# Attention scores from two float32r parts in 64-row tiles of the array, with the stacks loaded by GpSimd

## The reference, cut to what matters

```
Q = norm(x) @ Wq ; K = ctx @ Wk ; V = ctx @ Wv         (16 heads, d_k = 16)
scores = einsum('bhqd,bhkd->bhqk', Q, K) / sqrt(16)     (4 x 16 x 512 x 512)
attn = softmax(scores) ; out = einsum('bhqk,bhkd->bhqd', attn, V)
x = x + tanh(gate) * (out @ Wo)
```

## Time and profile before

| what | us |
|---|---|
| median of 3 runs | 898.56 (896.37 to 900.29) |
| profiled execution, its own time as the span from first to last instruction | 909.3 |
| PE busy, share of the span | 849.0, 93% |
| DVE busy | 618.8, 68% |
| ACT busy | 504.3, 55% |
| POOL busy | 161.1, 18% |
| steps of attention in layer 0 and layer 1, first `key_scores` to last `values` | 61.4 to 255, 518.3 to 715 |

### The profile page before, as it was taken

One profiled execution on the slowest core, in us unless ns is written; L12 is line 12 of the kernel. 1 busy time (PEld: TensorE's weight loads), 2 busy tenths in 40 slices (PEclk: granted clock), 3 DMA queues, 4 the chain that ended last, 5 costly groups with the idle time before them and its releaser, 6 DMA issues.

```text
span 909.3 us, 14428 instructions
## 1 busy us (share of the span) xinstructions
PE 849.0 (93%) x4542; PEld 474.4 (52%) x4543; DVE 618.8 (68%) x1207; ACT 504.3 (55%) x678; POOL 161.1 (18%) x283
## 2 busy tenths in 40 slices
PE   9999999999988999999968999999999989993398
PEld 6543333333468899999844433333334654441387
DVE  5898888888771222233248978888886578698942
ACT  4567777777731122222235667777777674597660
POOL 3241111111264000000151423000005303000000
PEclk9999999999999999999988999999999989997699
DMA  8898466654362111111469663333310000000011
GB/s 296 184 285 235 91 168 171 164 165 127 114 212 93 35 35 35 37 38 38 162 181 239 180 182 73 80 84 83 82 43 2 1 1 1 0 0 1 0 41 52
DMA packets 66558, 91.13 MB, mean 100 GB/s; under 512 B 24134, under 2 KB 50630, under 8 KB 66502
## 3 DMA queue, kind: packets, MB, share of 16 engines
q1 hardware_dynamic: 59196, 67.83, 29.0%
q0 software_dynamic: 5584, 19.93, 6.6%
q10 hardware_dynamic: 1728, 2.75, 0.8%
HBM read 62.64 MB, written 27.44 MB: 99 GB/s over the span
## 4 chain that ended last, share of the span: by engine, by line
PE 80%; DVE 8%; ACT 4%; issue 2%; DMA 2%; another core or an unknown queue 2%; SPq 1%; POOL 1%; DVEq 0%; ACTq 0%; POOLq 0%
PE PS L2197 13%; PE PS L2165 13%; PE PS L2186 12%; PE PS L2356 9%; PE PS L2422 8%; PE PS L2341 8%; PE PS L2443 5%; PE PS L2297 3%; PE PS L2148 1%; PE PS L2211 1%; PE PS L2128 1%; PE PS L2111 1%; PE PS L2175 1%; ACT BIG L1291 1%
## 5 line engine op out<-in xcount | busy, mean ns | idle before, releaser
L1571 DVE TENSOR_REDUCE MX<-PS 128x1 f32<-128x512 f32 x512 | 321.4, 684 | 44.3 <-PE PS L2165 43.6
L1148 ACT ACTIVATE Pt<-PS 128x1024 f32<-128x1024 f32 x256 | 248.1, 1021 | 101.6 <-PE PS L2186 100.7
L2165 PE MATMUL PS<-KSt,BIG 96*128 96x512 bf16 x512 | 175.4, 384 | 3.7 <-DVE bias_row L1458 2.7
L2186 PE MATMUL PS<-BIG,KSt 99*128 99x512 bf16 x512 | 150.5, 380 | 2.1 <-ACT Pt L1148 1.4
L2197 PE MATMUL PS<-Pt,VS 128*17 128x512 f32 x1024 | 137.0, 601 | 0.0
L2165 PEld LDWEIGHTS PS<-KSt,BIG 96*128 96x128 bf16 x512 | 40.6, 97 | 144.5 <-DVE MX L1571 87.3
L2341 PEld LDWEIGHTS PS<-KSt,Pt 128*128 128x128 f32 x736 | 85.6, 192 | 1.9 <-issue 0.8
L2341 PE MATMUL PS<-KSt,Pt 128*128 128x128 f32 x736 | 86.0, 275 | 0.7 <-issue 0.7
L1695 DVE COPY KSt<-PS 128x256 f32<-128x256 f32 x23 | 9.8, 425 | 111.1 <-PE PS L2328 111.1
L2422 PE MATMUL PS<-KSt,BIG 128*128 128x512 f32 x192 | 83.5, 596 | 0.0
L2186 PEld LDWEIGHTS PS<-BIG,KSt 99*128 99x128 bf16 x512 | 49.5, 98 | 56.3 <-ACT Pt L1148 4.9
(11 more groups left out here) (199 smaller groups left out, 1077.4 us busy)
## 6 DMA issues: line engine op xcount, KB each, us to landing
qk_parts<-BIG SPq DMA_DIRECT2D x64, 192.0 KB, 3.7
BIG<-in_w POOLq DMA_DIRECT2D x12, 1024.0 KB, 5.6
BIG<-qk_parts SPq DMA_DIRECT2D x32, 192.0 KB, 3.3
KSt<-qk_parts SPq DMA_DIRECT2D x32, 192.0 KB, 3.8
v_rows<-BIG SPq DMA_DIRECT2D x8, 544.0 KB
VS<-v_rows SPq DMA_DIRECT2D x32, 136.0 KB, 3.0
BIG<-qk_parts SPq DMA_DIRECT2D x32, 128.0 KB, 3.8
KSt<-qk_parts SPq DMA_DIRECT2D x32, 128.0 KB, 3.9
```

The lines of the kernel that those rows point to most:

```text
L1148: act.activation(PP[:, 2 * (kc % 2) + half, :, :].rearrange("p h t -> p (h t)"), ST[half], ACT.Exp, scale=DK ** -0.5).then_inc(exp_done, 1)
L1571: dve.tensor_reduce(MX[:, g % 2, i % TB, i // TB:i // TB + 1], ring(i), AX.X, ALU.max, negate=True).then_inc(max_taken, 1)
L2165: pe.matmul(ring(i), QS[0:ROWS, g, h, qc * P:(qc + 1) * P], KS[0:ROWS, g, h, :], start=True, stop=True).then_inc(max_done, 1)
L2186: last = pe.matmul(ST[half][:, i * S:(i + 1) * S], KS[0:ROWS + PARTS, g, h, kc * P:(kc + 1) * P], QS[0:ROWS + PARTS, g, h, :], start=True, ...
```

## The change

**Two parts instead of three.** Q and K are each kept as two float32r parts: the high part, which ACT writes as float32r, and the rest, which DVE writes as float32r in one instruction. The middle parts of ACT (32 instructions) and the low parts of POOL (26) and DVE (6) are gone. A stack has three pairs of parts, 48 rows, and two rows for the maximum, which is also split in two.

**Half of the array.** 50 rows fit into 64. Of the four heads of a group, heads 0 and 1 lie in partitions 0 to 63 and heads 2 and 3 in partitions 64 to 127, each matmul of `key_scores` and `max_scores` names its half with `tile_position`. The two heads of one ST buffer lie in the same half. `max_scores` takes the halves in turn (`half = i % 2`).

**Loads by POOL.** The stacks, the ones and the rows of the maxima are loaded by DMAs issued from POOL: eight a stack and two for the maxima. SP and ACT issue none of these now. POOL's loop over the sequences is written out. The stored parts are float32, 256 KB a store pair instead of 192 KB; a stack has 768 KB as before.

The diff, cut to its core:

```diff
...
-PARTS = 3
-ROWS = 6 * DK
-RUNS = [(0, 3), (3, 2), (5, 1)]
+PARTS = 2
+ROWS = 3 * DK
+HALF = P // 2
...
+            return PT[:, slot(kind, p, c), r, :]
+
+        STACK_IN = 8 * 16
+
+        def rows_of(half, first, count):
+
+            return slice(HALF * half + first * DK, HALF * half + (first + count) * DK)
+
+        def max_rows_at(half):
+
+            return slice(HALF * half + ROWS, HALF * half + ROWS + PARTS)
+
+        def head_of(i):
+
...
-            def load_stack(layer, b, g, some=range(len(RUNS))):
-                for first, k in [RUNS[i] for i in some]:
-                    dst = slice(first * DK, (first + k) * DK)
-                    for stack, which, parts in ((QS, 0, slice(0, k)), (KS, 1, slice(PARTS - k, PARTS))):
-                        run = qk_dram[layer, which, b, g, parts].rearrange("r (d h) t -> (r d) (h t)", h=G)
-                        sp.dma_start(stack[dst, g, :, :].rearrange("p h t -> p (h t)"), run).then_inc(q_stack[g], 16)
...
             def attention(layer):
-                for j in range(2 * KC):
-                    sp.wait_ge(part_out[j], 32 * B * (layer + 1))
                 sp.wait_ge(v_out, 16 * B * (layer + 1))
                 def batch(n, first, last):
                     for g in range(NG):
                         s = NG * n + g
                         if not last:
-                            sp.wait_ge(st_done, 8 * (s + 1))
-                            load_stack(layer, n + 1 - B * layer, g)
                             sp.wait_ge(pv_done, 4 * (s + 1))
                             load_v(layer, n + 1 - B * layer, g)
...
+                gp.wait_ge(ones_kept, 16)
+                load_ones()
+                first_stacks(0)
                 split_max(0, 0)
...
+            def load_stack(layer, b, g, half):
+                q, k = [qk_dram[layer, which, b, g].rearrange("r (d f h) t -> f r d (h t)", f=2, h=J)[half]
+                        for which in range(2)]
+                gp.dma_start(KS[rows_of(half, 0, 2), g, :, :].rearrange("p j t -> p (j t)"), k).then_inc(q_stack[g], 16)
+                gp.dma_start(QS[rows_of(half, 0, 2), g, :, :].rearrange("p j t -> p (j t)"),
+                             q[0].unsqueeze(0).to_broadcast([2, DK, J * S])).then_inc(q_stack[g], 16)
+                gp.dma_start(QS[rows_of(half, 2, 1), g, :, :].rearrange("p j t -> p (j t)"), q[1]).then_inc(q_stack[g], 16)
+                gp.dma_start(KS[rows_of(half, 2, 1), g, :, :].rearrange("p j t -> p (j t)"), k[0]).then_inc(q_stack[g], 16)
+
+            def load_stacks(layer, b, g):
+                for half in range(2):
+                    load_stack(layer, b, g, half)
+
+            def load_max_rows(n, g):
+
+                gp.wait_ge(max_copied, NG * n + g + 1)
+                gp.wait_ge(q_stack[g], STACK_IN * (n + 1))
+                for half in range(2):
+                    gp.dma_start(QS[max_rows_at(half), g, :, :],
+                                 MR[PARTS * J * TB * half:PARTS * J * TB * (half + 1), g % 2, :]).then_inc(max_rows[g], 16)
+
+            def parts_landed(layer, kind, c):
+                gp.wait_ge(part_out[slot(kind, 0, c)], landed(layer, kind, 0) + 32)
+
+            def first_stacks(layer):
+                for c in range(KC):
+                    parts_landed(layer, "k", c)
+                    parts_landed(layer, "q", c)
+                    load_stacks(layer, 0, 2 * c)
+                    load_stacks(layer, 0, 2 * c + 1)
...
+                s, top = NG * n + g, MX[:, g % 2, :, :].rearrange("p (f j) t -> p f j t", f=2)
                 gp.wait_ge(max_taken, 16 * (s + 1))
                 wait(gp, max_turned, s)
-                gp.tensor_tensor(MP[:, :, 0, :], MX[:, q, :, :], zero, ALU.subtract).then_inc(max_link, 1)
-                gp.wait_ge(max_link, 3 * s + 1)
-                gp.tensor_tensor(MD[:, :, :], MX[:, q, :, :], MP[:, :, 0, :], ALU.subtract).then_inc(max_link, 1)
-                gp.wait_ge(max_link, 3 * s + 2)
-                gp.tensor_tensor(MP[:, :, 1, :], MD[:, :, :], zero, ALU.subtract).then_inc(max_link, 1)
-                gp.wait_ge(max_link, 3 * s + 3)
-                gp.tensor_tensor(MP[:, :, 2, :], MD[:, :, :], MP[:, :, 1, :], ALU.subtract).then_inc(max_parts, 1)
+                gp.tensor_tensor(MP[:, :, 0, :, :].bitcast(F32R), top, zero, ALU.subtract).then_inc(max_link, 1)
+                gp.wait_ge(max_link, s + 1)
+                gp.tensor_tensor(MP[:, :, 1, :, :].bitcast(F32R), top, MP[:, :, 0, :, :], ALU.subtract).then_inc(max_parts, 1)
...
             def attention(layer, between):
 
+                for j in range(2 * KC):
+                    gp.wait_ge(part_out[j], 32 * B * (layer + 1))
+
                 def batch(n, first, last):
                     for g in range(NG):
                         if not (last and g == NG - 1):
                             split_max(n + (g + 1) // NG, (g + 1) % NG)
+                        fresh = g > 0 and not last or g == 0 and not first
+                        if fresh:
+                            gp.wait_ge(st_done, 8 * (NG * n + g))
+                            load_stacks(layer, n + (g > 0) - B * layer, (g - 1) % NG)
+                        if not (last and g == NG - 1):
+                            load_max_rows(n + (g + 1) // NG, (g + 1) % NG)
                         between(n, g, first, last)
-                over_batches(gp, layer, batch)
+                for b in range(B):
+                    batch(B * layer + b, b == 0, b == B - 1)
...
+            def low_part(layer, kind, p, c):
+
+                dve.wait_ge(hi_done, made(layer, kind, p, c) + 1)
                 if layer:
-                    dve.scalar_tensor_tensor(RB[:, c, :], qk_bank(c), bias_of(kind, c),
-                                             part_of(kind, p, c, 0), ALU.add, ALU.subtract).then_inc(r_done, 1)
+                    dve.scalar_tensor_tensor(part_of(kind, p, c, 1).bitcast(F32R), qk_bank(c), bias_of(kind, c),
+                                             part_of(kind, p, c, 0), ALU.add, ALU.subtract).then_inc(lo_done, 1)
                 else:
-                    dve.tensor_tensor(RB[:, c, :], qk_bank(c), part_of(kind, p, c, 0),
-                                      ALU.subtract).then_inc(r_done, 1)
-
-            def rests(layer, kind, p):
-
-                rest_of(layer, kind, p, 0)
-                rest_of(layer, kind, p, 1)
-
...
                 for i in some:
-                    h, qc = i // TB, i % TB
+                    half, j, qc = i % 2, i // 2 % J, i // G
+                    rows = rows_of(half, 0, ROWS // DK)
                     if i == 0:
-                        pe.wait_ge(q_stack[g], 96 * (n + 1))
+                        pe.wait_ge(q_stack[g], STACK_IN * (n + 1))
                     if i == 8 and max_before is not None:
                         pe.wait_ge(max_copied, max_before + 1)
                     elif i == 14 and out_before is not None:
                         pe.wait_ge(o_ready, out_before + 1)
                     else:
                         wait(pe, max_taken, 16 * (NG * n + g) + ring_before(i))
-                    pe.matmul(ring(i), QS[0:ROWS, g, h, qc * P:(qc + 1) * P], KS[0:ROWS, g, h, :],
-                              start=True, stop=True).then_inc(max_done, 1)
+                    pe.matmul(ring(i), QS[rows, g, j, qc * P:(qc + 1) * P], KS[rows, g, j, :], start=True, stop=True,
+                              tile_position=(HALF * half, 0)).then_inc(max_done, 1)
...
 
@@ -2171,20 +2079,19 @@
                 pe.wait_ge(max_parts, s + 1)
                 if ahead is not None:
                     pe.wait_ge(max_taken, 16 * ahead + 4)
-                for t in range(TB):
-                    last = pe.transpose(to[0:PARTS * G, t * P // 2:(t + 1) * P // 2].bitcast(BF16),
...
             def key_scores(s, n, g, kc, half):
 
                 if kc == 0 and half == 0:
-                    pe.wait_ge(max_rows[g], 16 * (n + 1))
+                    pe.wait_ge(max_rows[g], 32 * (n + 1))
                 wait(pe, exp_done, 2 * (4 * s + kc) + half - 1)
-                for i in range(2):
-                    h = 2 * half + i
-                    last = pe.matmul(ST[half][:, i * S:(i + 1) * S], KS[0:ROWS + PARTS, g, h, kc * P:(kc + 1) * P],
-                                     QS[0:ROWS + PARTS, g, h, :], start=True, stop=True)
+                rows = slice(HALF * half, HALF * half + ROWS + PARTS)
+                for j in range(J):
+                    last = pe.matmul(ST[half][:, j * S:(j + 1) * S], KS[rows, g, j, kc * P:(kc + 1) * P],
+                                     QS[rows, g, j, :], start=True, stop=True,
+                                     tile_position=(HALF * half, 0))
                 last.then_inc(st_done, 1)
 
...
```

More of the change, by code:

```diff
@@ L27 @@
 F32 = mybir.dt.float32
+F32R = mybir.dt.float32r
 BF16 = mybir.dt.bfloat16
@@ L82, in build_program @@
         PS = ctx.enter_context(nc.psum_tensor("PS", [P, 8, 512], F32))
```

(20 more changed lines are left out.)

242 lines of the change are left out of this document (58 added, 184 removed).

## The result

The changed kernel took 973.9 us (median of 4 runs, 954.7 to 992.1) against 898.0 before: 1.070 times as long, 95% interval 1.062 to 1.077. The changed kernel is slower, and outside the predicted range of 862 to 930 us. The profiled run is the fastest of the four; the others had a lower mean clock of PE, 0.89 to 0.93 against 0.95, where the kernel before had 0.98.

The account below looks back on a forecast made before the run. PE was taken to bound the kernel, DVE close behind, and POOL's late maxima to set most steps after the change. Steps -20.2 us plus preparation +7.9 gave -12.3, hence 885 us, range 862 to 930.

Parts of the forecast that it names:

- The chain over two steps: Attention steps with stacks: matmuls for the maxima, DVE, POOL's split, ten issues and landing sum to 22.5 us, 11.25 a step.
- a landing of 2.1 us: Last term of the two-step sum: time for the DMA of the maxima to land before the next step's key_scores.
- Issues of POOL: Small direct DMA issues back to back on POOL, ten a step with stacks: 0.80 us each, between bounds 0.74 and 1.28.
- The rival of POOL's issues: POOL's stack issues ahead of the maxima become the bound: 913 us at 1.0 us an issue, 956 at 1.28; chance 15%.
- the rival without overlap: Matmuls in different halves of the array run one after another: +15 us, 914 us; chance 13%.
- half pace: Rival: float32r matmuls on PE take 0.435 us instead of 0.22, giving steps of 15.6 us and 1,030 us; chance 14%.
- 0.44 us a quarter: PE's score matmuls in a step: halves side by side turn eight 0.22 us slots into six, 1.76 us a step.
- I take 10.8: Step length in us set by PE (10.3) and DVE (10.5), with the ring of three banks between them.
- Preparation: Work ahead of the attention steps: mode switches, loads of ones, waits for stores, together +7.9 us.
- Hidden, by under 2 us: Preparation, layer 0: POOL's first four stacks, 32 DMAs, done at 50 us, before the turn due at 52.4.
- 0.1 us each: Loss on PE at each tile-mode change; 46 changes in layer 0's preparation cost 4.6 us, less 1.3 for side-by-side pairs.
- Nothing for the middle and low parts: Preparation: removing these instructions on ACT, POOL and DVE, which stand beside matmuls of busy PE, costed at nothing.

Follow-up runs that it names:

- e5: Changed kernel with the stack's repeated-source DMA cut into two DMAs of 16 rows, still issued by POOL: 928 us, 1.034 times the kernel before.
- e8: e6 with DVE reducing only 256 of the 512 keys of each max_scores result: 890 us, 0.989 times the kernel before.
- e4: e3 with the two heads of one score buffer in different halves of the array: 957 us, 1.068 times the kernel before.
- e12: Kernel before the change, with DVE reducing only 256 of 512 keys for the maximum: 895 us, 0.996 times the kernel before.
- e6: e3 with the repeated-source DMA cut in two; SP loads the stacks, ACT the rows of the maxima: 926 us, 1.029 times the kernel before.
- e7: e6 with score matmuls over the whole array, summing two heads' scores, so not computing the attention: 931 us, 1.037 times the kernel before.
- e1: Changed kernel with ACT instead of POOL issuing the two DMAs of the rows of the maxima: 962 us, 1.069 times the kernel before.
- e3: Changed kernel with all loads back on SP and ACT at their old places, both ends named float32: 961 us, 1.072 times the kernel before.
- e2: Changed kernel with both ends of POOL's DMAs named float32, so that none converts: 978 us, 1.091 times the kernel before.

## Why the prediction was wrong

*Landing of the rows of the maxima: the step that failed.* The chain over two steps has "a landing of 2.1 us". It is 2.1 to 8.3 us from 130 to 245 us in layer 0, and 9.8 once. The 2.1 us came from a DMA over 128 partitions with no stack ahead of it; neither the eight stack DMAs in front nor the repeated source in two of them has a term in the sum. The forecast's own sign of being wrong, "maxima that land much later than 2 us behind their issue", came true. Instead of steps of 11.3 us, 0.65 less than before, layer 0 had steps of 11.8 to 16.5, 13.0 in the median. Cutting that DMA gave back 32 to 46 us of the whole (e5); of the profiled run it gave 11 in prep 1 and 13 in the steps of layer 0.

*That was not all.* e5 still takes 928 us, 43 more than the forecast of 885. By its profile about 30 of them are the steps (10 us more than before in the two spans of 15 steps, where 20 less were forecast), and about 14 the preparations (7.5 and 14.1 us lost, where 7.9 were forecast).

*Issues of POOL: priced too high.* 0.80 us was taken, 0.52 measured. The rival of POOL's issues took the right place, the rows of the maxima late for `key_scores`, for the wrong reason.

*Halves: the mechanism was right, the size was not.* The two halves do overlap, so the rival without overlap falls, and with a distance of 0.24 us so does half pace. "0.44 us a quarter" measured 0.13 (2.82 to 2.69), and "I take 10.8" for a step that PE and DVE set measured 11.8. PE and DVE were each bounded alone; the chain through three banks was not drawn (e8, e4, e12).

*Preparation: failed.* "Hidden, by under 2 us" was 6 us late: the part stored at 22.6 landed at 28.0 instead of 24, and the first stack needed until 41.6 from its first issue at 28.5, beside SP's stores, with DMA engines 0.88 busy. "0.1 us each" for a change of mode was 0.2: a lone score matmul costs 0.40 us more. For 23 groups that would be 9.2 us, twice the 4.6 of the forecast, yet all of prep 1 is just 3.3 us longer in e6 than in e7, where e7 waits 1.2 us for DVE at its end; what else wins it back is open. The 0.1 came from the gap ahead of `values`.

*The clock: not in the sum.* All terms were at the full clock. In the profiled run it was at half from 38 to 59 us, and prep 2 took 13.4 us more than before at a mean clock of 0.72. Why a busy PE stays at half so long is open.

*Nothing for the middle and low parts: nothing speaks against it.* Up to the first `max_scores` of layer 1 two parts take 241.2 us and three parts 240.2 (e12). In e7, with two parts and no halves, both preparations are 0.4 to 2.6 us longer than with three (before and e12), but e7 differs from them in the loads too.

## What to carry to other kernels

Read the first dimension of every DMA's pattern, repetitions too: a 2 there kept a 128 KB load on two engines, and small, urgent DMAs came late behind it, from the same queue and from another (e1, e3). Where two engines hand banks to each other, sum one way round through both; their separate totals are only lower bounds. A tile mode that pays in a dense loop can lose elsewhere: keep its matmuls in groups, and count the clock.

## What the runs showed of the hardware beyond that

PE at 1.2 GHz for 51 us with 51.78 of 51.80 us busy (e6), and for 3.4 us with whole-array matmuls in the same order (e7): a busy PE does not always get its clock back at once. A float32r matmul over 512 columns follows the one before on its half or on the whole array by 0.23 to 0.24 us (bfloat16 0.22), and its weight load takes 0.19 against 0.10 us. Leaving out the conversion from float32 to float32r in POOL's DMAs won nothing (e2). Matmuls in the upper half of the array started ahead of one in the lower half that the program has before them.
